# Moving VectorE's attention sums of graphs 2 and 3 behind the statistics of the second norm

## What is computed

```python
si = x @ attn_w[l, :d]
sj = x @ attn_w[l, d:]
scores = si[:, :, None] + sj[:, None, :] + attn_b[l]
scores = jnp.where(scores >= 0, scores, 0.2 * scores)
scores = jnp.where(mask, scores, -jnp.inf)
attn = jax.nn.softmax(scores, axis=-1)
agg = jnp.einsum('bij,bjd->bid', attn, x)
h = layernorm(x + agg, g1[l], beta1[l])
ff = gelu(h @ W1[l] + b1[l]) @ W2[l] + b2[l]
x = layernorm(h + ff, g2[l], beta2[l])
```

## Time and profile before

| what | value |
|---|---|
| median of 3 runs | 1709.91 us (1709.25 to 1709.99) |
| the profiled execution | 1712.13 us, its span 1710.3 us |
| busy: TensorE / VectorE / ScalarE / GpSimd | 94% / 77% / 72% / 78% of the span |
| mean granted TensorE clock | 0.98 of full speed |
| graph network, steps 1 to 13 and 17 to 29 | a step every 25.89 us |
| layer 2, steps 33 to 44 | a step every 26.78 us |

### The profile page before, as it was taken

How to read it: one execution, slowest core, us unless ns; L and a number is a source line. 1 busy time by engine, 2 the same in 40 slices (tenths; PEclk the granted TensorE clock), 3 DMA queues, 4 the chain that set the end, 5 groups by cost and what they waited for, 6 DMA issues and landing times.

```text
span 1710.3 us, 40177 instructions
## 1 busy us (share of the span) xinstructions
PE 1609.1 (94%) x11904; PEld 1425.8 (83%) x11904; DVE 1320.2 (77%) x5300; ACT 1230.9 (72%) x2855; POOL 1337.6 (78%) x2385
## 2 busy tenths in 40 slices
PE   4999999984999999999999999999999999999994
PEld 3888888872898998998898998988889888888894
DVE  1898898896777777777977777777888887888862
ACT  1888888883677677677777777776776777777763
POOL 5688888875478777787787787787778999999996
PEclk8999999996999999999999999999999999999997
DMA  6122332232022122122122221221220212222211
GB/s 200 64 93 93 98 98 90 87 106 80 26 99 91 44 74 74 37 74 73 38 75 72 88 74 38 72 74 37 74 73 26 86 65 95 74 74 79 69 50 49
DMA packets 145979, 127.50 MB, mean 75 GB/s; under 512 B 16512, under 2 KB 136832, under 8 KB 145920
## 3 DMA queue, kind: packets, MB, share of 16 engines
q1 hardware_dynamic: 138880, 124.30, 22.5%
q10 hardware_dynamic: 7040, 2.51, 0.6%
HBM read 89.04 MB, written 37.75 MB: 74 GB/s over the span
## 4 chain that ended last, share of the span: by engine, by line
PE 56%; POOL 13%; DVE 5%; issue 2%; ACT 1%; POOLq 0%; DVEq 0%; ACTq 0%
PE ps L45 24%; PE ps L894 24%; PE ps L866 4%; PE ps L880 2%; DVE gnn_junk L1026 2%; POOL xo L807 2%; POOL gnn_n L160 2%; POOL gnn_norm L801 2%; POOL gnn_fin L821 2%; POOL gnn_norm L160 2%; POOL inv L155 1%; PE ps L858 1%; POOL gnn_hb L790 1%; PE ps L873 1%; POOL gnn_hb L786 1%
## 5 line engine op out<-in xcount | busy, mean ns | idle before, releaser
L894 PE MATMUL ps<-gnn_w_hi,gnn_g_hi 128*128 128x256 f32 x1536 | 433.9, 282 | 0.0
L894 PE MATMUL ps<-gnn_w_lo,gnn_g_hi 128*128 128x256 f32 x1536 | 428.9, 279 | 0.0
L894 PE MATMUL ps<-gnn_w_hi,gnn_g_lo 128*128 128x256 f32 x1536 | 428.7, 279 | 0.0
L993 ACT ACTIVATE gnn_g_hi<-ps,b_cols 128x512 fp32r<-128x512 f32 x384 | 264.3, 688 | 200.1 <-PE ps L45 200.1
L1097 DVE TENSOR_TENSOR gnn_g_lo<-ps,gnn_g_hi 128x512 fp32r<-128x512 f32 x384 | 262.4, 683 | 101.6 <-ACT ps L994 101.0
L45 PE MATMUL ps<-gnn_hT_hi,gnn_w_hi 128*128 128x512 f32 x768 | 338.4, 441 | 0.0
L45 PE MATMUL ps<-gnn_hT_hi,gnn_w_lo 128*128 128x512 f32 x768 | 303.5, 395 | 0.0
L45 PE MATMUL ps<-gnn_hT_lo,gnn_w_hi 128*128 128x512 f32 x768 | 303.4, 395 | 0.0
L894 PEld LDWEIGHTS ps<-gnn_w_lo,gnn_g_hi 128*128 128x128 f32 x1536 | 288.9, 188 | 2.2
L894 PEld LDWEIGHTS ps<-gnn_w_hi,gnn_g_hi 128*128 128x128 f32 x1536 | 288.8, 188 | 2.2
L894 PEld LDWEIGHTS ps<-gnn_w_hi,gnn_g_lo 128*128 128x128 f32 x1536 | 288.7, 188 | 0.0
(11 more groups left out here) (127 smaller groups left out, 3979.4 us busy)
## 6 DMA issues: line engine op xcount, KB each, us to landing
hist<-xo SPq DMA_DIRECT2D x48, 512.0 KB, 3.9
x<-hist SPq DMA_DIRECT2D x48, 512.0 KB, 3.8
aw<-in_L_gnn_attn_w SPq DMA_DIRECT2D x48, 256.0 KB, 4.1
gmask<-mask_hist SPq DMA_DIRECT2D x48, 256.0 KB, 4.1
att_xT_raw<-in_xT SPq DMA_DIRECT2D x16, 512.0 KB, 3.3
att_xl<-in_x SPq DMA_DIRECT2D x16, 512.0 KB, 3.6
gnn_fin<-hist SPq DMA_DIRECT2D x16, 512.0 KB, 3.8
out<-gnn_fin SPq DMA_DIRECT2D x16, 512.0 KB, 3.0
```

Source lines behind the costliest of these rows:

```text
L894: mm = e.matmul(FF2[j % 2], g[a][:, m, j * N:(j + 1) * N], W2[b][:, m, :], start=(n == 0), stop=(n == len(terms) - 1))
L993: e.activation(g[0][:, m, :], FF1[FFB[m]], ACT.Gelu, bias=bias)
```

## The change

The attention sums of graphs 2 and 3 of step t+3 leave their place between `hT_lo` and `stats2` and stand behind the means of `mv2`, as VectorE's last work of the step. Nothing else is changed; no wait is added or removed in the text.

```diff
                     residual2(t, par, 2)
                     if more >= 1:
                         hT_lo(t1)
-                    if more >= 3:
-                        attention_sums(t3, p3, h3, 2)
-                        attention_sums(t3, p3, h3, 3)
                     for j in range(3):
                         stats2(t, j)
                     residual2(t, par, 3)
@@
                     for j in range(GROUP):
                         ins = e.bn_aggr(mv2[:, j, :], st2[:, j, :])
                     ins.then_inc(mv2_out, 1)
+                    if more >= 3:
+                        attention_sums(t3, p3, h3, 2)
+                        attention_sums(t3, p3, h3, 3)
```

## The result

The changed kernel takes **1712.68 us** (median of 22 runs, 1711.67 to 1714.46); the kernel before, run beside it, 1710.07 (1709.25 to 1712.72). The ratio is 1.0015, 95% interval 1.0008 to 1.0021: 2.6 us slower. That is less than the 0.2% that was called a difference beforehand, but the interval leaves out 1, so it is a small loss and not a gain. Forecast was 1708.8, 1.1 faster.

The account below looks back on a forecast made before the run. TensorE was taken to bound layers 0 and 1, a ring through mv2 layer 2. -9.7 us there and +8.6 from collisions in layers 0 and 1 gave -1.1: 1708.8 us on the median 1709.91, range 1701 to 1717.

Parts of the forecast that it names:

- Part 1: Layer 2: moving the sums lets the last residual start 2.31 us earlier, TensorE binds next; -9.7 us over 11 steps.
- the ring of layer 2: Loop from mv2 through GpSimd's norms, TensorE's transposes and VectorE's last residual to the next mv2: 26.78 us a step, TensorE 25.89.
- Part 2: Layers 0 and 1: the last residual and mv2 come 1.29 us earlier, which by itself gains nothing.
- Part 3: Layers 0 and 1: earlier GpSimd collides with sums ahead of probs_max, delaying TensorE 0.32 us a step, +8.6 us in 27 steps.
- the collision: GpSimd's L786 and VectorE's sums of graphs 0 and 1 take turns, about 0.88 us a sum instead of 0.35.
- the prediction's own sign of being wrong: Layers 0 and 1: the prediction fails if L786 doesn't start 1.1 to 1.3 us earlier relative to TensorE.
- The rule for the four sums: Ahead of probs_max: first sum waits for L786's first graph, three follow at 0.885; 2.95 us in step 19, 3.24 in step 20.
- rival B: Layers 0 and 1: the collision outweighs the gain, delay about 0.6 us a step, +6.5 us, 1716.4; chance 0.28.
- A: Rival: only layer 2's gain counts, collision delay under 0.2 us a step; 1700.2 to 1705.6 us; chance 0.24.
- C: Rival: in layer 2 GpSimd's own work grows and binds at 26.2, gain only 6.6; 1711.9 us; chance 0.08.
- D: Rival: VectorE is late at gelu_lo, needing 0.54 us more than counted; chance 0.01.
- rival E: Layers 0 and 1: a colliding sum and L786 cost their full length, 1.05 us; +22.0, 1722.2 us; chance 0.01.

Follow-up runs that it names:

- e1: Kernel before, with the sums of graphs 2 and 3 moved only in layer 2 (steps from 33 on): 1700.87 us, ratio 0.9938.
- e5: Changed kernel, with the sums of graphs 2 and 3 left out in the bodies of steps 0 to 31: 1713.76 us, ratio 1.0018 to the kernel before.
- e6: Changed kernel plus one useless 128x4 power on GpSimd behind its wait for mv2 in steps 0 to 31: 1703.10 us, ratio 0.9955 to the kernel before.
- e4: Kernel before, with probs_max and residual2 of graph 1 put ahead of the sums of graphs 0 and 1 in layers 0 and 1: 1716.04 us, ratio 1.0036.
- e3: Changed kernel, with probs_max and residual2 of graph 1 ahead of the sums of graphs 0 and 1: 1701.39 us, ratio 0.9955 to the kernel before.
- e9: Kernel before, sums moved only in layer 2, plus two GpSimd powers behind the mv2 wait in steps 0 to 31: 1715.05 us, ratio 1.0026.

## Why the prediction was right or wrong

- **Part 1, the ring of layer 2: right.** -9.83 us for a forecast of -9.7; TensorE is next with 25.87, and GpSimd's wait for mv2 is gone. e1 shows it alone.
- **Part 2, the earlier mv2 in layers 0 and 1: right.** 1.29 was forecast, 2.76 - 1.49 = 1.27 measured. Nothing came of it by itself, and VectorE's next gelu kept its idle time.
- **Part 3, the collision: right mechanism, mis-sized.** The step that failed is "I allow 0.15 for being held up there, so 1.14". From mv2 to L786 it is 15.18 us in step 19 where it was 14.82: 0.36 more, of which L153 and L155 make 0.31. So L786 moved by 0.91, and the prediction's own sign of being wrong, a start not 1.1 to 1.3 earlier relative to TensorE, came true. It starts 0.41 and 0.11 ahead of the first sum, not 0.64 and 0.35. The rule for the four sums held: with these starts it gives 3.18 and 3.48, measured are 3.18 and 3.49 to 3.50. It isn't exact further out: at -0.67 (step 14 of the changed kernel) it gives about 2.92, and 3.01 were measured, and e5 has the second outcome of 3.6. For the result, what I had wrong is the input. A smaller shift is worse here, as the first sum meets more of L786. The delay is 0.44 and 0.62, mean 0.53, in place of 0.32: 13.76 us in the 26 steps between the layers' ends, in place of 8.6 for 27.
- **A term left out.** For steps 14, 15 and 30 to 32 I counted nothing; the layers' ends gained 1.56 in all. VectorE splits the next layer's weights there (L1121), with two inputs too, beside GpSimd's L790. First step 14 of the kernel before, then of the changed one:

```profile
817.07 4.54 DVE L1121 TENSOR_TENSOR gnn_w_lo<-w_raw,gnn_w_hi 128x512 fp32r<-128x512 f32 x4
```

```profile
821.82 3.88 DVE L1121 TENSOR_TENSOR gnn_w_lo<-w_raw,gnn_w_hi 128x512 fp32r<-128x512 f32 x4
```

GpSimd is further on, less of L790 collides, and the split is 0.66 shorter; h's low part, for which TensorE waits there, comes that much earlier: the wait of the weight load of L858 goes from 1.21 to 0.58 in step 15, and from 1.24 to 0.58 in step 31. The same collision that costs in front of probs_max pays back here.
- **The sum**: -9.83 + 13.76 - 1.56 = +2.4 and the last steps' -0.1, where -9.7 + 8.6 stood. The sign hung on the mean delay against 9.7 / 27 = 0.36, which the text named as the point from which rival B decides; 0.53 is past it. Of the rivals, B had this right, the start "less shifted", with a chance of 0.28, though its size (0.6 a step, 1716.4) was too large. The forecast's own stretch, 1705.6 to 1713.4, has 1712.7 in it, but by luck: it stands for a delay of 0.2 to 0.49, and 0.53 would give 1714.5; the layers' ends, which it left out, bring the time back. A, C and D did not come; for C, GpSimd's small operations in layer 2 are stretched too (L155 to 1.19), but L790 is relieved.
- **Rule against row.** The Trainium skill (SBUF — State Buffer, "Who interferes with whom" and the reading of its diagram) has the loser of the shared port pair block for the whole instruction. The 0.88 us from sum to sum, now in nearly all of them, is still under 1.05, the full length of both; by rival E the time would have been 1722.2.

**Still open**: which of its two outcomes the case with L786 at -0.71 takes (e5) was not tried by itself. Nor is it shown why a power that stands first isn't stretched beside the moved sums (1.03 in e6) while L153 and L155 of the changed kernel are.

## What to carry to other kernels

An instruction moved off one path makes another engine earlier, and that engine's work falls on other work: look for what it will run beside before counting the gain as free. If one place of a stage has a different bound (layer 2 here), make the move there alone: that was worth 10 us, the whole move lost 2.6. Work ahead of a signal that another engine needs should be work that can't be slowed by a third; but look where it goes instead, as e4 lost 6 us by the same swap that e3 gained by.

## What the runs showed of the hardware

- GpSimd's operations of 128x4 are stretched by VectorE's sums: L153 0.23 to 0.40, L155 1.04 to 1.18. A power of the same size that stands first takes 1.03 beside them, and L152 behind it 0.25.
- VectorE's sums lose little beside GpSimd's scalar pass (L160), 1.83 us for four where undisturbed ones start 0.35 apart, and stretch it from 2.17 to 3.13, and the same sums beside its passes with two inputs (L786, L790) go at 0.88 in place of 0.35. Added work of 2 us on GpSimd in each of 32 steps turned 2.6 us over the kernel before into 12.7 under it.
- TensorE's granted clock fell from full to half (0.50) for about 3.4 us behind waits of 1.91 and 2.12 us in e4 and of 2.45 us in e9. It didn't fall behind waits of 1.89 us in e4 and of 2.46 us in e9.
